# The cms down projection as seven products over pairs of chunks, with the weights' block sums built in DRAM

## What is computed

```python
attn_out = jnp.einsum('btT,bTd->btd', attn, v) @ Wp + bp
cms_out = jax.nn.gelu(attn_out @ cW1 + cb1, approximate=False) @ cW2 + cb2
cms_out = cms_out + target_embed
concat = jnp.concatenate([attn_out, cms_out], axis=-1)
modifier = jax.nn.gelu(concat @ mW1 + mb1, approximate=False) @ mW2 + mb2
out = jnp.clip(x + cms_out + modifier, 0.0, 1.0)
```

## Time and profile before

| | |
|---|---|
| median of 3 runs | 2157.76 us (2157.53 to 2160.55) |
| the profiled execution, its own time | 2156.44 us |
| its span on the core | 2154.8 us |
| PE busy | 2105.6 us, 98% |
| DVE / ACT / POOL busy | 71% / 48% / 28% |
| matmuls | 9256 (128 of them transposes) |
| DMA | 146.41 MB, mean 68 GB/s |

### The profile page before, as it was taken

The page is one execution under the profiler, slowest core; times in us unless marked ns, Lnnn a source line. Parts: engine busy times, 40 slices in busy tenths (PEclk is TensorE's granted clock), DMA queues, the critical chain, the costliest instruction groups (busy, mean ns, idle before and its releaser), DMA issues.

```text
span 2154.8 us, 24846 instructions
## 1 busy us (share of the span) xinstructions
PE 2105.6 (98%) x9256; PEld 1724.7 (80%) x9256; DVE 1537.7 (71%) x1923; ACT 1042.1 (48%) x1527; POOL 598.7 (28%) x620
## 2 busy tenths in 40 slices
PE   8999999999999999999999999999999999999997
PEld 6888887888788887888877888788887888878884
DVE  4366678776867668876776766977686866787676
ACT  5264445454446444544554544444454644454444
POOL 1001136452001113655000111655400011355420
PEclk9999999999999999999999999999999999999999
DMA  8101131212202112221312111321130211311211
GB/s 304 40 10 59 59 88 49 59 48 78 100 20 88 59 59 69 59 59 59 116 41 88 40 59 42 96 59 59 40 127 20 102 46 59 88 50 59 59 59 39
DMA packets 125767, 146.41 MB, mean 68 GB/s; under 512 B 5952, under 2 KB 100160, under 8 KB 123728
## 3 DMA queue, kind: packets, MB, share of 16 engines
q1 hardware_dynamic: 122912, 130.05, 18.9%
q0 software_dynamic: 1504, 8.49, 1.9%
q10 hardware_dynamic: 1232, 6.29, 0.7%
HBM read 123.84 MB, written 12.58 MB: 63 GB/s over the span
## 4 chain that ended last, share of the span: by engine, by line
PE 85%; DVE 10%; ACT 2%; issue 2%; DMA 0%; SPq 0%; ACTq 0%; DVEq 0%
PE bank L615 28%; PE bank L617 28%; PE bank L616 28%; DVE ring L1321 2%; DVE vc L1363 2%; DVE pc L1493 1%; DVE xa L1358 1%; DVE lsum L1695 1%; ACT ring L955 1%; ACT raw L1098 0%; PE bank L923 0%; DVE xs L1700 0%; DVE xs L1653 0%; DVE xs L1685 0%; DVE raw L1439 0%
## 5 line engine op out<-in xcount | busy, mean ns | idle before, releaser
L1321 DVE TENSOR_TENSOR ring<-stage,ring 128x1024 fp32r<-128x1024 f32 (+1 forms) x312 | 363.4, 1176 | 103.8 <-ACT ring L955 103.6
L551 POOL TENSOR_TENSOR stage<-stage 128x256 f32<-128x256 f32 x120 | 106.3, 886 | 1122.1 <-DMA stage<-cms_w 904.5
L615 PE MATMUL bank<-ph_hi,ring 128*128 128x512 f32 x1048 | 410.6, 392 | 5.4 <-issue 2.4
L617 PE MATMUL bank<-ph_hi,ring 128*128 128x512 f32 x1048 | 407.9, 389 | 0.0
L616 PE MATMUL bank<-ph_lo,ring 128*128 128x512 f32 x1048 | 407.9, 389 | 0.0
L615 PE MATMUL bank<-xa,ring 128*128 128x512 f32 x1016 | 396.0, 390 | 2.9 <-DVE xs L1653 2.1
L617 PE MATMUL bank<-xa,ring 128*128 128x512 f32 x1016 | 395.3, 389 | 0.0
L616 PE MATMUL bank<-xa,ring 128*128 128x512 f32 x1016 | 395.3, 389 | 0.0
L955 ACT ACTIVATE ring<-stage 128x1024 fp32r<-128x1024 f32 (+1 forms) x312 | 296.3, 970 | 111.7 <-PE bank L617 78.3
L615 PEld LDWEIGHTS bank<-ph_hi,ring 128*128 128x128 f32 x1048 | 196.7, 188 | 53.7 <-issue 7.2
L617 PEld LDWEIGHTS bank<-ph_hi,ring 128*128 128x128 f32 x1048 | 196.7, 188 | 41.0
(11 more groups left out here) (159 smaller groups left out, 3139.6 us busy)
## 6 DMA issues: line engine op xcount, KB each, us to landing
stage<-mod_w SPq DMA_DIRECT2D x128, 256.0 KB, 3.4
stage<-cms_w SPq DMA_DIRECT2D x36, 512.0 KB, 3.6
stage<-mod_w SPq DMA_DIRECT2D x32, 512.0 KB, 4.9
stage<-cms_w SPq DMA_DIRECT2D x56, 256.0 KB, 4.3
fold_staging<-fold_w SPq DMA_DIRECT2D x16, 512.0 KB, 5.2
stage<-folded SPq DMA_DIRECT2D x16, 512.0 KB, 4.3
xs<-pc POOLq DMA_DIRECT2D x8, 1024.0 KB, 8.3
stage<-ada_w SPq DMA_DIRECT2D x16, 512.0 KB, 3.6
```

Source lines behind the costliest of these rows:

```text
L551: pool.tensor_tensor(part(S1), part(S2), part(A22), ALU.add).then_inc(sums_ready, 1)
L615: pe.matmul(dst, lh, rh, start=start and n == 0, stop=False, skip_group_check=not start)
L617: done = pe.matmul(dst, ll, rh, start=False, stop=n == last, skip_group_check=not start)
L1321: dve.tensor_tensor(ring_part(key, 1), staged(key), f32(ring_part(key, 0)), ALU.subtract).then_inc(w_lo, 1)
```

## The change

**Pairs.** The down projections of the chunks 0 to 5 are made in three pairs (`paired`, `PAIRS`), each by the seven products of one 2 x 2 block product with 512 hidden features, as 7 products of 12 matmuls (`pair_product`). Chunks 6 and 7 keep the plain form. The cms slots 1 to 6 have new lists, `pair_odd` and `pair_even`, slot 7 `cms_last`. POOL makes the sums T1 to T4 of the paired hidden tiles (`pair_sum`, 8 a pair). `raw_odd` holds the odd chunk's tiles, in space of `vc`. The down weights of a pair are one piece "E" of seven blocks of 128x512, in two stage buffers at once; all "A" pieces now use stage 0.

**Block sums in DRAM.** The block sums of the up pieces of chunks 1 to 7, of the three E pieces and of chunk 8's two up pieces (A, C) are no longer made by POOL in the stage. For each of the two layers 12 such pieces of seven blocks are laid out in DRAM (`ready_up`, `ready_pair`): SP issues seven DRAM-to-DRAM copies a piece (`prepare`), POOL issues three accumulating DMAs (`sum_once`) and then two more (`sum_twice`). `load_ready` then loads all seven blocks. Layer 0's are made at the start, once the folds are written; layer 1's between the modifier slots of rounds 0 and 1.

```diff
+            def load_ready(key):
+
+                layer = key[0] // 2
+                n, at = READY_IN[(layer, *key[1:])], STAGE_OF[key]
+                src, _ = ready_piece(layer, *key[1:])
+                to = stage_pair if key[1] == "E" else stage[at]
+                sp.wait_ge(w_lo, STAGE_FREE[key])
+                sp.wait_ge(prepared[n], 16 * 2 * len(BATCHES_READY[n]))
+                sp.dma_start(to[:, :, :], src.rearrange("b p n -> p b n")).then_inc(stage_in[at], 16)
+
+            def prepare(batch):
+
+                for layer, kind, n in BATCHES_READY[batch]:
+                    to, at = ready_piece(layer, kind, n)
+                    for block, m, k in ((A11, 0, 0), (A12, 0, 1), (S4, 0, 1), (S1, 1, 0), (S3, 1, 0), (S2, 1, 1), (A22, 1, 1)):
...
+                        sp.dma_start(to[at[block], :, :].rearrange("p (k n) -> p k n", k=2), src[:, :, m, :]).then_inc(copied[batch], 16)
...
                 load((r, "P"), cms_w[2 * (r // 2) * CH, :, :])
+                if r == 0:
+                    sp.wait_ge(fold_out[1], 16 * LAYERS)
+                    for batch in range(EARLY - 1):
+                        prepare(batch)
                 load_up(r, 1)
-                load_down(r, 0)
+                load_pair(r, 1)
+                if r == 0:
+                    prepare(EARLY - 1)
...
+            def sum_once(batch):
+
+                pool.wait_ge(copied[batch], 16 * COPIES * len(BATCHES_READY[batch]))
+                for piece in BATCHES_READY[batch]:
+                    w, at = ready_piece(*piece)
+                    for block, more in ((S1, A22), (S3, A11), (S4, A22)):
+                        pool.dma_start(rows(w, at[block]), rows(w, at[more]), accum_op=ALU.add,
+                                       max_dma_last_dim=8192).then_inc(summed_once[batch], 16)
+
+            def sum_twice(batch):
+
+                pool.wait_ge(summed_once[batch], 16 * 3 * len(BATCHES_READY[batch]))
+                for piece in BATCHES_READY[batch]:
+                    w, at = ready_piece(*piece)
+                    for block in (S2, S4):
+                        pool.dma_start(rows(w, at[block]), rows(w, at[S3]), accum_op=ALU.add,
+                                       max_dma_last_dim=8192).then_inc(prepared[batch], 16)
...
+            for batch in range(EARLY):
+                sum_once(batch)
+                if batch:
+                    sum_twice(batch - 1)
+            sum_twice(EARLY - 1)
             for r in range(ROUNDS):
-                for n in range(1, CH + 1):
-                    sums((r, "A", n))
-                sums((r, "C", CH))
+                for n in range(1, CH):
+                    i = n // 2
+                    if n % 2 and paired(n):
+                        pair_sum(r, i, T1, 0)
+                        pair_sum(r, i, T1, 1)
+                        for j in range(2):
+                            pair_sum(r, i, T3, j)
+                            pair_sum(r, i, T2, j)
+                    elif n % 2 == 0:
+                        pair_sum(r, i - 1, T4, 0)
+                        pair_sum(r, i - 1, T4, 1)
...
+            def pair_even(r, n):
+                i = n // 2 - 1
+                up(r, n, Q5)
+                up(r, n, Q1)
+                pair_product(r, i, Q3)
+                up(r, n, Q6)
+                up(r, n, Q2)
+                up(r, n, Q3)
+                up(r, n, Q7)
+                pair_product(r, i, Q6)
+                up(r, n, Q4)
```

More of the change, by code:

```diff
@@ L156, in staged_up @@
     def staged_up(r, n):
[L157 removed]
+        pieces.append(((r, "A", n), 0))
         if n >= CH:
@@ L458, in load_up @@
                 layer = r // 2
-                if n < CH:
-                    load((r, "A", n), cms_w[2 * (layer * CH + n), :, :])
+                if n <= CH:
+                    load_ready((r, part, n))
                 else:
@@ L844, in down, with pair_product @@
                          (lambda k: pe.wait_ge(h_lo, hidden_at(r, n, k))) if b == 0 and m == 0 else None)
+            def pair_product(r, i, q):
+                blk, at = OPERAND[q], RING_E[q] * BLK
+                pe.wait_ge(w_lo, W_AT[r, "E", 2 * i + 1, PAIR_GROUP[q]])
+                pe.wait_ge(h_lo, pair_split_at(r, i, blk, 1))
+                before = {Q6: Q1, Q7: Q6, Q4: Q7, Q3: Q5, Q2: Q3}
+                if q in before:
+                    pe.wait_ge(added, pair_down_at(r, i, before[q]))
+                elif i:
+                    pe.wait_ge(added, pair_down_at(r, i - 1, Q4 if q == Q1 else Q2))
+                two = pair[int(q in (Q5, Q3, Q2))]
+                for j in range(2):
+                    tile(two[:, j, :], [(ring[:, 0, at + k * BLK + j * P:at + k * BLK + (j + 1) * P],
+                                         ring[:, 1, at + k * BLK + j * P:at + k * BLK + (j + 1) * P],
+                                         pair_hi(blk, k), pair_lo(blk, k)) for k in range(2)],
+                         down_done if j else None, start=q in (Q1, Q5, Q2))
@@ new lines, in pair_add @@
+            def pair_add(r, i, q):
+                b, m = DRAIN[q]
+                acc, src = pc[:, b, m:m + 2, :], pair[int(q in (Q5, Q3, Q2))]
+                minus = q in (Q5, Q7, Q4)
+                dve.wait_ge(down_done, pair_down_at(r, i, q))
+                if q not in PAIR_FIRST_DRAIN:
+                    dve.wait_ge(added, pair_down_at(r, i, {Q2: Q1, Q6: Q3, Q7: Q5}[q]))
+                elif i:
+                    dve.wait_ge(added, pair_down_at(r, i - 1, PAIR_LAST_DRAIN[b, m]))
+                if i == 0 and q in PAIR_FIRST_DRAIN:
+                    dve.wait_ge(attn_lo, (r + 1) * ATT_BUILDS)
+                    for j in range(2):
+                        done = dve.tensor_scalar(acc[:, j, :], src[:, j, :], -1.0 if minus else 1.0,
+                                                 cbias[:, 2 * r + b, m + j:m + j + 1], ALU.mult, ALU.add)
+                elif minus:
+                    done = dve.tensor_tensor(acc, acc, src[:, :, :], ALU.subtract)
+                else:
+                    done = dve.tensor_tensor(acc, src[:, :, :], acc, ALU.add)
+                done.then_inc(added, 1)
@@ L1593, in slot @@
-                up_lo(r, n + 1, 1)
-                if not last:
-                    for m in range(1, KT):
-                        down_add(r, n - 1, 1, m)
+                for m in range(KT):
+                    down_add(r, n - 1, 1, m)
+                hidden_lo(r, n, 3)
+                split_lo((r, "C", n + 1, 0))
+                hidden_lo(r, n, 1)
+                combine(r, n, C12)
+                hidden_lo(r, n, 2)
+                split_lo((r, "A", n + 1, 1))
+                split_lo((r, "C", n + 1, 1))
```

494 lines of the change are left out of this document (386 added, 108 removed).

## The result

| | before | after |
|---|---|---|
| median (runs measured together) | 2157.65 us (2155.94 to 2160.55) | 2143.23 us (2142.51 to 2146.78) |
| the profiled execution, its span | 2156.44, 2154.8 | 2146.78, 2145.1 |
| ratio of times | | 0.9935 [0.9918, 0.9952] |

The change gains 14.4 us, and the forecast of 2143 is met. The parts behind it are not all as forecast, and the experiments show why. The profiled execution of after is the longest of its four (the others have spans of 2140.8 to 2141.6), so its own balance comes out smaller than that of the medians: 9.7 us. For the profiled execution the forecast was 2141.3, and that is missed by 5.5 us.

The account below looks back on a forecast made before the run. The PE, busy 98%, was taken to bound the kernel: 2156.4 - 32.6 (matmuls) + 3.5 (pair slots) + 14 (start) = 2141.3 us profiled, median 1.3 above at 2143 us; range 2124 to 2190.

Parts of the forecast that it names:

- Step 1: Pairs of chunks down: 84 matmuls a pair instead of 96, 144 fewer at 0.2267 us, -32.6 us.
- slot-8 stall: PE wait at the cms part's end, beside POOL's chunk 9 sums: 2 to 3 us a round, said to stay.
- Step 2: Steady pair slots: no stall found, margins 0.4 to 2 us; allowance of 0.3 us for each of 12 pairs, +3.5 us.
- step 4: Larger loads, layer 1's copies and POOL's issues, the cms part's end: all put at no cost.
- Step 3: Start of round 0: DRAM copies, sums and loads take 110 us, POOL free at 173 instead of 159.2, +14 us.
- The first to be late is therefore POOL: Start of round 0: A1 lands at about 130, wanted at 138.7, so POOL, 14 us late, is the first late.
- The lower rate for copies: DRAM-to-DRAM copies at start: 210 GB/s instead of 270 would mean lateness 28 us and a change worth nothing.
- DRAM on both sides: Rival at the start: copies and sums at upper-bound rates, POOL 63 us late, 2192 us; chance 0.23.
- the even slots that don't fit: Rival in pair slots: DVE and POOL stretch each other, 24 slots lose a microsecond each, 2167 us; chance 0.07.
- The full gain: Rival at the start: DRAM work hides whole, lateness 0 to 4 us, 2129 us; chance 0.18.

Follow-up runs that it names:

- after_again: The changed kernel, unaltered, run once more beside the other kernels: 2143.63 us, ratio 0.9923 to before.
- late_five: Changed kernel with layer 0's fifth batch (A8, C8) copied behind slot 2's loads and summed from slots 3 and 4: 2142.03 us, ratio 0.992 to before.
- pool_sums: Changed kernel with the pairs kept but nothing made in DRAM, all block sums made by POOL in the stage: 2170.31 us, ratio 1.0053 to before.
- spread2: The spread kernel with batch five copied behind slot 5's load instead of slot 4's: 2132.98 us, ratio 0.9875 to before.
- spread: Changed kernel with only batches 1 and 2 made before round 0, batch 3 behind E1's load, 4 and 5 behind slots 2 and 4's: 2135.12 us.
- copies_only: Changed kernel without layer 0's accumulating DMAs, pieces loaded once their copies landed, result not the reference's: 2130.82 us, one execution.
- ready_nine: The spread2 kernel with chunk 9's two up pieces (A9, C9) also built in DRAM: 2124.55 us, ratio 0.984 to before.

## Why the prediction was right, and where not

**Step 1, matmuls.** Right: 144 fewer, 168 matmuls a pair at 0.2267 us. From round 0's first adapter load to round 3's last it was 1582.4 us before and is 1561.3 now: three rounds and 21.1 us, 7.0 a round where 8.16 were to go. The 3.4 us between go with the slot-8 stall, which after has in two of these rounds: after_again, with one, takes 1558.6, late_five, with three, 1563.1. But pool_sums shows a condition that the step left out: the gain is there only because the sums went to DRAM. The prediction priced the DRAM part as a cost of the start alone and put its use at nothing; it is what leaves POOL and the DVE room.

**Step 2, the pair slots.** The term was mis-sized: +3.5 was forecast for 12 pairs, measured is 0 (38.10 us, the PE never idle). The walk, which found no stall with margins of 0.4 to 2 us, was right, and the allowance on top of it was not needed. A loss of about this size came elsewhere, at slot 8. There had shown how DVE and POOL stretch each other, and the prediction let the stall "stay" in step 4. In the profiled execution that failed: the row of `vc` has 5.0 us, where before's has 1.4. But the kernels' profiles have the stall in one round of four (before, after_again, spread2), two (spread), three (after, copies_only), four (late_five) and none (ready_nine), so that the change itself makes it larger isn't shown; what is shown, by ready_nine, is that it goes with POOL's sums.

**Step 3, the start.** Forecast 14. Up Q3 of slot 1 started at 178.71 where 163.0 was the mark, 15.7 late, and 2.1 us went to the half clock behind it: 17.7. By the step's own parts: POOL free at 173.84 in place of 159.2 is 14.6; its two sums, the splits and `take` took 4.9 us to the PE where 3.8 were allowed, 1.1; the clock 2.1 (with rounding). So POOL's time was right within a microsecond (173 forecast), partly by luck: SP's first copy went out at 60.3 and not at 63.3, the copies moved 250 to 261 GB/s alone, not 270, and the accumulating queue 28.16 MB in 7.2% of 16 engines' 2145 us, 182 GB/s, not 207. At these rates the sum is 54 + 51 + 8 + 6 = 119 us, an estimate; measured are 113.5, so by this sum the two queues overlap by some 6.

"The first to be late is therefore POOL" is wrong. A1 was said to land at 130 and was split at 149.6, 10.9 later than in the earlier trace rows. The 61 us for the transfers ahead of it fit the load's issue (60.3 + 61 is 121.3, it was issued at 122.7), not its landing. What failed is the amount of sums ahead of A1. The step counted 3.5 MB of them; the trace has A1 landing right behind the last sums of batches one to four, 8.5 MB by the step's own counting (five sums a piece, 0.131 MB each for seven A pieces, 0.262 for three E pieces). With these, at the step's rates, 60.3 + 44 + 41 is 145, an estimate, and 149.6 was measured. That it is the sums, and not the copies issued behind it, is shown: 26.9 us to land in late_five, which has no copies behind A1, but 5.2 and 8.2 in copies_only and spread, which have copies behind and few sums or none beside it. Together with the folds (0.7) and smaller waits this puts the PE 8.0 us behind in slot 1 (at 166.5, against the same matmul of before), the 3.0 us wait and 2.9 us of half clock among them. It adds nothing to the 17.7, since POOL's gate comes later and would hold the PE until 178.7 in any case. A gate taken away lays bare the one ahead of it: late_five still has A1's, spread has neither.

The clock was not in the step at all. It costs twice, 2.9 us that POOL's gate hides, and 2.1 that show.

**Step 4, edits at nothing.** Loads of 0.9 and 1.8 MB beside the PE: held, DMA share 0.28 in a pair and no wait. Layer 1's copies and sums in slots 8 to 13: no wait names them. The slot-8 stall is the exception told above.

**The lower rate for copies.** The prediction named 207 to 214 GB/s between HBM tensors (the Trainium skill, DMA: Bandwidth & Descriptors, section "Latency and other measured facts") as what would make the change worth nothing. In copies_only the copies move 248 to 261 GB/s. The measurement decides: that price doesn't hold for these copies, which differ in shape from the ones that the Trainium skill measured (short runs into contiguous pieces, there [128 x 16 KiB] tiles), though it isn't far off.

**The sum.** For the profiled execution: -32.6 of matmuls, 0 in the pairs, +17.7 at the start and +5.2 behind it (3.4 in rounds 1 to 3, the rest in round 0), so -9.7, which is what its span shows. Of the 5.2 the rows of the slot-8 stall hold 3.6 (5.0 less before's 1.4). Against the forecast of the profiled execution that is 3.7 us too little at the start and 5.2 unforeseen, less 3.5 too much in the pairs: with rounding, the 5.5 that it missed. By medians the change gains 14.4, and there the total was hit with errors that cancel: the pairs against the start, while the slot-8 stall, which ranges from 1.7 to 6.7 us in the profiles of after, after_again and late_five, falls short in most executions if after_again's profile stands for them. That part is luck. Of the rivals, DRAM on both sides (2192) falls by copies_only's rates, the even slots that don't fit (2167) by the pair's row, but pool_sums shows that this rival's mechanism decides when the sums stay on POOL. The full gain's place (2129) is nearly reached by copies_only's one execution, and passed by ready_nine.

## What stays open

Why the slot-8 stall is there in one round or in four in executions of nearly the same kernel isn't settled: the rows show that the DVE's operations take 1.2 or 1.8 us as POOL's fall beside them, not what shifts them. Open too is how much of the pair's length in pool_sums is POOL's list and how much the DVE's longer instructions, and what ready_nine would gain with its `sum_once` moved behind the T4 sums, since it still waits 3.1 us for ACT in round 0.

## What to carry to other kernels

Sums of weights that are used more than once can be built once in DRAM by DMAs: here this gained more by taking the additions off POOL (with them on POOL the DVE's list of 32 us took 37 and the kernel 27 us longer) than it cost at the start. Put such preparation in the order of its need, the first pieces ahead of the first load and the rest behind later loads: a load that was issued amid the accumulating DMAs landed only with the last of them. The issuing of DMAs also has a place in an engine's list: ahead of a sum that others wait for, six issues of 4.7 us held the PE up by 1.5. When an engine's list is costed, ask also who runs beside it, at the rates of a stretch in which both do.

## What of the hardware was not expected

- After an idle of 3.0 us, and again of 6.3 us, the PE ran at the lower clock level (0.50 granted, 0.43 us a matmul) for some 6 and 4 us: the first wait cost 2.9 us on top of its 3.0, the second 2.1 on top of 6.3.
- A load of 0.9 MB took 26.9 us to land beside accumulating DMAs (after, late_five), 5.2 without them (copies_only), though 14 copies were issued right behind it in both after and copies_only.
- DVE additions of 128x1024 take 1.76 us beside POOL's sums and 1.22 without; four TENSOR_SCALARs 4.25 us in place of 4 x 0.54.
- Copies from DRAM to DRAM in runs of 512 B and 1 KB run at 248 to 261 GB/s at a DMA share of 0.87 to 0.90, as fast as loads with the same runs (256).
- The issuing engine can be held by its own issues: SP took 33.0 us for 14 copies beside POOL's sums (124.65 in its timeline), 13.5 us for the same 14 in copies_only, and 4.84 us for the first seven. That it is a full queue that holds it is our reading; no run tests it.
